# Half tiles of x2 instead of whole tiles between the counts of the dst tiles

## The chip, the cores and the metric

The kernel runs on one core of one Trainium2 chip. The time is the device time of one execution in microseconds (us), as the median of several runs; lower is better. A profile of one execution stands beside it.

## The reference, cut to what matters

A graph layer over N = 1250 nodes with D = 1024 features and E = 20000 edges, sorted by dst:

```
xn = layernorm(x)
x  = x + gnn(xn, W, a, src, dst) + mix(xn, ...)[0]
x  = x + ffn(layernorm(x), ...)[0]

gnn: h = xn @ W;  e = exp(-leaky_relu(al[src] + ar[dst]))
     h'[n] = sum over edges with src == n of e * h[dst], divided by the sum of e
mix: x2 = layernorm(xn, ln1_g, ln1_b)
     q, k, v = x2 @ wq, x2 @ wk, x2 @ wv; a linear attention on cos and sin features, then its own ffn
```

The change lies in the first stage. It does two things that have nothing to do with each other but share the engines. It counts, for each pair (dst, src), how many edges there are (the gnn sums are later made as dense products with these counts), and it makes x2, transposed and split in a high and a low part for the products with wv, wk and wq.

## The kernel before, in words

The stage is `count_and_second_norm`. Nodes are in NT = 10 tiles of T = 125. Each engine has its own instruction stream, written out by hand, and semaphores tie them.

Counting. Edges are in 160 chunks of 125. For dst tile t, only the chunks that may hold a dst of this tile are gone through, in a loop that takes HOT = 3 chunks a turn. For each chunk VectorE (DVE) writes a one-hot of the src (`hot_s`, L399, 125x1250) and a one-hot of the dst within the tile (`hot_d`, L401), in one of three slots, after waiting on `s_used` that the slot is free. TensorE (PE) waits on `s_hot` for the chunk and multiplies the two in three matmuls (L468) that add up in `p_cnt[t % 2]`, three PSUM banks; this frees the slot (`s_used`). Three matmuls with zero operands open the sums (L461) and three close them (L472, `s_tile`). ScalarE (ACT) then copies the counts out in three pieces (`keep_counts`, L300, `s_kept`), and SyncE stores them.

x2. ACT has normalised the rows into `xr` (L305, `s_z`). For node tile i, PE transposes eight 125x128 blocks (L451) into `p_t`, which has two PSUM banks: blocks 0 to 3 go to bank 0, blocks 4 to 7 to bank 1 (`s_t` after each bank). ACT applies gain and bias, four activations per bank (`affine`, L316), into `x2[i % 2]` (`s_x2` after each bank), and copies the whole tile rounded as the high part (L321, `s_hi`). DVE subtracts for the low part (`keep_lo`, L387, `s_lo`). PE may write a bank again when `affine` has read it:

```
if i:
    pe.wait_ge(s_x2, 2 * i - 1 + half)
```

and `affine(i)` waits for `keep_lo(i - 2)`, whose buffer it takes.

Order. A table says which node tiles are transposed after the count of dst tile t:

```
AFTER = {0: (), 1: (0,), 2: (1, 2), 3: (3, 4), 4: (5,), 5: (6,), 6: (7,), 7: (8,), 8: (9,), 9: ()}
```

PE does `count_tile(t)`, then the transposes of `AFTER[t]`. ACT does `keep_counts(t)`, then `affine` of each tile of `AFTER[t]`, then waits for the next count. DVE does the one-hots of tile t, then `keep_lo` of the tiles of `AFTER[t - 1]`, then the one-hots of t + 1. "Gap t" below is the time between the chunks of dst tile t and those of t + 1.

After tile 9, ACT and DVE finish the last x2 tile and a barrier ends the stage; the products with wv, wk and wq (L1468) follow.

Of the kernel before, what the change touches and what calls it, by code (L numbers as in the profile page):

```python
# [6 lines left out]
ACT = mybir.ActivationFunctionType  # L7
# [10 lines left out]
T = 125  # L18
NT = N // T
T16 = T // 16 * 16  # L20
MOVED = 32
K8 = D // 128
# [106 lines left out]
def count_and_second_norm(core):  # L129
# [3 lines left out]
    x2_hi, x2_lo = core.x2_hi, core.x2_lo  # L133
    with ExitStack() as ctx:  # L134
# [6 lines left out]
        xr = sb("x_rows", [T, NT, D])  # L141
# [65 lines left out]

        RSTD_STEPS = 26

        AFTER = {0: (), 1: (0,), 2: (1, 2), 3: (3, 4), 4: (5,), 5: (6,), 6: (7,), 7: (8,), 8: (9,), 9: ()}  # L210

        block = ctx.enter_context(nc.Block())

# [68 lines left out]
        @block.scalar  # L282
        def _(act):
            def first_stats(i):
                col = slice(i, i + 1)
                act.wait_ge(s_x[i], MOVED)
                act.wait_ge(s_stat, 3 * i)
                act.activation(junk[:], xr[:, i, :], ACT.Identity, accum_out=core.mean[:, col]).then_inc(s_stat, 1)
                act.wait_ge(s_stat, 3 * i + 1)
                act.mul(core.negmean[:, col], core.mean[:, col], -1.0 / D).then_inc(s_stat, 1)  # L290
                act.wait_ge(s_stat, 3 * i + 2)
                act.activation(junk[:], xr[:, i, :], ACT.Square, bias=core.negmean[:, col],
                               accum_out=core.var[:, col]).then_inc(s_stat, 1)

            def keep_counts(t):
                act.wait_ge(s_tile, t + 1)
                if t >= 2:
                    act.wait_ge(s_cst[t % 2], MOVED * (t // 2))
                for n, (a, w) in enumerate(THIRDS):
                    last = act.activation(kept(t)[:, a:a + w], p_cnt[0:T, t % 2, n, 0:w], ACT.Copy)  # L300
                last.then_inc(s_kept, 1)

            def normalise(i):
                col = slice(i, i + 1)
                act.activation(xr[:, i, :], xr[:, i, :], ACT.Identity, scale=core.ln_scale[:, col],  # L305
                               bias=core.ln_shift[:, col]).then_inc(s_z, 1)

            def affine(i):
                if i >= 2:
                    act.wait_ge(s_lo, i - 1)  # L310
                for k in range(K8):
                    if k % 4 == 0:
                        act.wait_ge(s_t, 2 * i + k // 4 + 1)
                    g = core.cols[:, COLUMN_AT["L0_mix_ln1_g"].start + k:COLUMN_AT["L0_mix_ln1_g"].start + k + 1]
                    b = core.cols[:, COLUMN_AT["L0_mix_ln1_b"].start + k:COLUMN_AT["L0_mix_ln1_b"].start + k + 1]
                    last = act.activation(x2[:, i % 2, k, :], p_t[:, k // 4, (k % 4) * T:(k % 4 + 1) * T], ACT.Identity,  # L316
                                          scale=g, bias=b)
                    if k % 4 == 3:
                        last.then_inc(s_x2, 1)
                act.wait_ge(s_x2, 2 * i + 2)  # L320
                act.activation(x2_hi[:, :, i * T:(i + 1) * T], x2[:, i % 2], ACT.Copy).then_inc(s_hi, 1)  # L321

            for i in range(NT):
                first_stats(i)
            keep_counts(0)
            act.wait_ge(s_rstd, RSTD_STEPS)
            for i in range(NT):
                normalise(i)
                if i == 3:
                    keep_counts(1)  # L330
            act.wait_ge(s_gb, 1)
            for t in range(2, NT):
                for i in AFTER[t - 1]:
                    affine(i)
                keep_counts(t)
                if t == NT - 2:
                    for which in range(3):
                        act.wait_ge(core.mix_loaded[which], 16)
                        act.activation(core.mix_hi[which][:], core.mix_in[which][:], ACT.Copy).then_inc(core.mix_hi_ready[which], 1)

        @block.vector
        def _(dve):
# [46 lines left out]
            with dve.register("chunks_done") as done, dve.register("first_chunk") as r0, dve.register("past_chunk") as r1:  # L389
                dve.reg_mov(done, 0)  # L390

                def tile_onehots(t):
                    first, past = groups_of(dve, t, (r0, r1))
                    with dve.Fori(first, past, HOT) as g:
                        before = dve.snap(done, min_val=0, max_val=NT * (CHUNKS + HOT))
                        for j in range(HOT):
                            dve.wait_ge(s_used, before + j + 1)
                            at = bass.ds(g + j, 1)
                            dve.tensor_scalar(hot_s[:, j, :], iota_h[:], ends[:, at, 0:1].rearrange("p a b -> p (a b)"), None,  # L399
                                              ALU.is_equal)  # L400
                            dve.tensor_scalar(hot_d[:, j, 0:T], iota_t[:, t, 0:T], ends[:, at, 1:2].rearrange("p a b -> p (a b)"),  # L401
                                              None, ALU.is_equal).then_inc(s_hot, 1)
                        dve.reg_add(done, done, HOT)

                tile_onehots(0)
                dve.wait_ge(s_vt, 1)
                dve.tensor_copy(core.cols[:], p_cols[:, 0:COLUMN_COUNT]).then_inc(s_gb, 1)
                tile_onehots(1)
                for t in range(2, NT):
                    for i in AFTER[t - 2]:  # L410
                        keep_lo(i)
                    tile_onehots(t)
                for i in AFTER[NT - 2]:
                    keep_lo(i)
                dve.wait_ge(core.mix_hi_ready[VALUE], 1)
                dve.tensor_tensor(core.mix_lo[VALUE][:], core.mix_in[VALUE][:], f32(core.mix_hi[VALUE][:]),
                                  ALU.subtract).then_inc(core.mix_lo_ready[VALUE], 1)

        @block.tensor
        def _(pe):  # L420
# [18 lines left out]
            pe.wait_ge(s_zero, 2)  # L439
            pe.wait_ge(s_span, 1)  # L440

            def transposes(i):
                pe.wait_ge(s_z, i + 1)
                if i == 0:
                    pe.wait_ge(s_gb, 1)
                for half in range(2):
                    if i:
                        pe.wait_ge(s_x2, 2 * i - 1 + half)
                    for n in range(4):
                        k = 4 * half + n  # L450
                        last = pe.transpose(p_t[:, half, n * T:(n + 1) * T], xr[:, i, k * 128:(k + 1) * 128], ident[0:T, 0:T])  # L451
                    last.then_inc(s_t, 1)

            with pe.register("chunks_done") as done, pe.register("first_chunk") as r0, pe.register("past_chunk") as r1:
                pe.reg_mov(done, 0)

                def count_tile(t):
                    if t >= 2:
                        pe.wait_ge(s_kept, t - 1)
                    for n, (a, w) in enumerate(THIRDS):  # L460
                        pe.matmul(p_cnt[0:T, t % 2, n, 0:w], zeros[:], zero_rows[:, 0:w], start=True, stop=False)  # L461
                    first, past = groups_of(pe, t, (r0, r1))
                    with pe.Fori(first, past, HOT):
                        before = pe.snap(done, min_val=0, max_val=NT * (CHUNKS + HOT))
                        for j in range(HOT):
                            pe.wait_ge(s_hot, before + j + 1)
                            for n, (a, w) in enumerate(THIRDS):
                                last = pe.matmul(p_cnt[0:T, t % 2, n, 0:w], hot_d[:, j, 0:T], hot_s[:, j, a:a + w], start=False, stop=False)  # L468
                            last.then_inc(s_used, 1)
                        pe.reg_add(done, done, HOT)  # L470
                    for n, (a, w) in enumerate(THIRDS):
                        last = pe.matmul(p_cnt[0:T, t % 2, n, 0:w], zeros[:], zero_rows[:, 0:w], start=False, stop=True)  # L472
                    last.then_inc(s_tile, 1)

                count_tile(0)
                pe.wait_ge(core.vectors_loaded, 16 * len(COLUMNS))
                pe.transpose(p_cols[:, 0:COLUMN_COUNT], core.vectors[:], ident[0:COLUMN_COUNT, 0:COLUMN_COUNT]).then_inc(s_vt, 1)
                for t in range(1, NT):
                    count_tile(t)
                    for i in AFTER.get(t, ()):  # L480
                        transposes(i)


def node_features(core):
# [2005 lines left out]
```

## Time and profile before

| | |
|---|---|
| time, median of 3 runs | 1284.93 us (1282.96 to 1285.98) |
| the profiled execution, its own time | 1283.55 us |
| its span in the profile | 1281.8 us |
| PE busy | 1196.6 us, 93% of the span |
| DVE busy | 756.2 us, 59% |
| ACT busy | 705.5 us, 55% |
| counting stage | up to about 156 us of the span |

The span starts with the first instruction of the profile. In timelines each row has its start, its duration, engine, line, and in brackets how long the engine had been idle and who ended that. PEld is the load of weights on TensorE, which overlaps its matmuls.

### The profile page before, as it was taken

How to read it: one execution, taken by the hardware profiler on the slowest of the kernel's cores; microseconds unless marked ns; L12 is line 12 of the kernel's file. 1: busy time of each engine (PE TensorE's matmuls, PEld its weight loads, DVE VectorE, ACT ScalarE, POOL GpSimd, SP SyncE). 2: the span in 40 equal slices, each digit the busy share in tenths (PEclk: the TensorE clock that was granted, in tenths of full speed). 3: DMA queues.
4: the chain of work that ended last, by engine and by line, in shares of the span. 5: the costliest groups of instructions: out<-in, count | busy, mean ns of one | idle time of the engine just before them, and what ended most of it. 6: DMA issues, size and time to landing. Idle time of an engine off the chain costs nothing. (4 is left out here: it accounts for less than half of the span.)

```text
span 1281.8 us, 19485 instructions
## 1 busy us (share of the span) xinstructions
PE 1196.6 (93%) x6857; PEld 1050.0 (82%) x6857; DVE 756.2 (59%) x1244; ACT 705.5 (55%) x1069; POOL 338.4 (26%) x296
## 2 busy tenths in 40 slices
PE   6989889999999999999559998899999998999997
PEld 4555689999999999999547876899988786887884
DVE  7988815656565666656543664777755122556646
ACT  8275628777777777777755432322245432355544
POOL 1500004242332324242111110266653332111100
PEclk9999999999999999999759999899998999999999
DMA  8001220022020202021145452522244332711103
GB/s 215 10 20 29 46 77 1 18 53 69 0 69 0 69 0 69 4 65 64 55 150 168 159 167 95 186 84 85 84 118 158 97 96 60 221 44 47 34 19 97
DMA packets 72194, 99.41 MB, mean 78 GB/s; under 512 B 27241, under 2 KB 52165, under 8 KB 71631
## 3 DMA queue, kind: packets, MB, share of 16 engines
q1 hardware_dynamic: 68684, 86.11, 23.1%
q0 software_dynamic: 3456, 12.58, 3.2%
q8 instruction: 34, 0.56, 0.2%
q14 instruction: 20, 0.16, 0.0%
HBM read 77.04 MB, written 21.63 MB: 77 GB/s over the span
## 5 line engine op out<-in xcount | busy, mean ns | idle before, releaser
L1146 POOL TENSOR_TENSOR cos_sin_lo<-cos_sin,cos_sin_hi 125x1024 fp32r<-125x1024 f32 (+1 forms) x40 | 95.4, 2384 | 248.6 <-ACT cos_sin_hi L1234 248.6
L468 PE MATMUL p_cnt<-hot_s,hot_d 125*125 125x418 bf16 x540 | 112.7, 359 | 1.8 <-DVE hot_d L401 1.8
L705 PE MATMUL p_h<-x 128*125 128x512 f32 x400 | 110.3, 403 | 0.0
L399 DVE TENSOR_SCALAR hot_s<-iota_h,ends 125x1250 bf16<-125x1250 f16 x180 | 97.6, 542 | 14.4 <-PE p_cnt L468 12.3
L1468 PE MATMUL p_w<-x,mix_hi_v 128*128 128x416 f32 (+1 forms) x384 | 105.2, 355 | 0.0
L468 PEld LDWEIGHTS p_cnt<-hot_s,hot_d 125*125 125x125 bf16 x540 | 62.4, 138 | 51.5 <-DVE hot_d L401 41.4
L1468 PE MATMUL p_w<-x,mix_hi_q 128*128 128x416 f32 (+1 forms) x384 | 104.2, 352 | 0.0
L1468 PE MATMUL p_w<-x,mix_hi_k 128*128 128x416 f32 (+1 forms) x384 | 104.1, 352 | 0.0
L966 PE MATMUL rows_in_psum<-h_hi,a_lo 125*125 125x342 f32 x300 | 96.7, 322 | 2.7 <-DVE a_lo L910 2.7
L966 PE MATMUL rows_in_psum<-h_lo,a_hi 125*125 125x342 f32 x300 | 96.7, 322 | 0.0
L966 PE MATMUL rows_in_psum<-h_hi,a_hi 125*125 125x342 f32 x300 | 96.7, 322 | 0.0
L705 PEld LDWEIGHTS p_h<-x 128*125 128x125 f32 x400 | 75.4, 190 | 18.3
L1234 ACT ACTIVATE cos_sin_hi<-cos_sin 125x1024 fp32r<-125x1024 f32 (+1 forms) x80 | 83.6, 1045 | 7.0 <-PE p_kv_at L1549 4.8
L1376 DVE TENSOR_SCALAR whole_turns<-p_p 125x512 f32<-125x512 f32 (+1 forms) x80 | 54.6, 682 | 40.2 <-PE p_p L1519 35.3
L1800 PE MATMUL rows_in_psum<-wo_rest,at_hi 128*125 128x512 f32 x280 | 76.8, 396 | 0.0
L1219 ACT ACTIVATE cos_sin<-part_turn 125x512 f32<-125x512 f32 (+1 forms) x80 | 49.9, 623 | 48.8 <-DVE part_turn L1378 47.9
L1468 PEld LDWEIGHTS p_w<-x,mix_hi_v 128*128 128x128 f32 x384 | 73.1, 191 | 0.8
L1468 PEld LDWEIGHTS p_w<-x,mix_hi_q 128*128 128x128 f32 x384 | 72.1, 188 | 0.9
L1468 PEld LDWEIGHTS p_w<-x,mix_hi_k 128*128 128x128 f32 x384 | 72.2, 188 | 0.6
L1468 PE MATMUL p_w<-x,mix_lo_v 128*128 128x416 f32 (+1 forms) x192 | 69.0, 359 | 3.5 <-PEq L134 3.5
L1468 PE MATMUL p_w<-x,mix_lo_q 128*128 128x416 f32 (+1 forms) x192 | 67.6, 352 | 0.0
L1468 PE MATMUL p_w<-x,mix_lo_k 128*128 128x416 f32 (+1 forms) x192 | 67.6, 352 | 0.0
(297 smaller groups left out, 3055.6 us busy)
## 6 DMA issues: line engine op xcount, KB each, us to landing
x_in<-in_x_dram SPq DMA_DIRECT2D x30, 448.0 KB
attn_dram<-attn_t SPq DMA_DIRECT2D x8, 625.0 KB, 3.9
at_in<-attn_dram SPq DMA_DIRECT2D x10, 500.0 KB, 4.6
x_rows<-in_x_dram SPq DMA_DIRECT2D x10, 448.0 KB
x_in<-gnn_dram SPq DMA_DIRECT2D x10, 448.0 KB
out_dram<-rows SPq DMA_DIRECT2D x10, 448.0 KB
mix_in_v<-in_L_mix_wv_dram SPq DMA_DIRECT2D x8, 512.0 KB, 6.0
mix_in_k<-in_L_mix_wk_dram SPq DMA_DIRECT2D x8, 512.0 KB, 4.7
```

The lines of the kernel that those rows point to most:

```text
L399: dve.tensor_scalar(hot_s[:, j, :], iota_h[:], ends[:, at, 0:1].rearrange("p a b -> p (a b)"), None, ALU.is_equal)
L468: last = pe.matmul(p_cnt[0:T, t % 2, n, 0:w], hot_d[:, j, 0:T], hot_s[:, j, a:a + w], start=False, stop=False)
L705: last = pe.matmul(p_h[0:T, i % 2, n, :], left[i % 2][:, k, :], right[:, k, cols], start=(k == 0 and m == 0), stop=(k == K8 - 1 and m == 2))
L966: last = pe.matmul(p_o[0:T, i % 2, n, 0:H_COLS], left[:, i % 2, d, :], right[:, d, cols], start=(d == 0 and m == 0), stop=(d == NT - 1 and ...
L1146: pool.tensor_tensor(full(cs_lo, k), full(cs, k), f32(full(cs_hi, k)), ALU.subtract).then_inc(s_cslo[0], 1)
L1219: act.activation(step_view(cs, k, 1), rows(part, k), ACT.Sin, scale=TWO_PI)
L1234: act.activation(full(cs_hi, k), full(cs, k), ACT.Copy).then_inc(s_cshi, 1)
L1376: dve.tensor_scalar(flat(whole, k), flat(p_p, k), MAGIC, -MAGIC, ALU.add, ALU.add).then_inc(s_whole, 1)
L1468: last = pe.matmul(p_w[:, n, 0:w], left[which][:, k, :], right[:, k, a:a + w], start=(k == 0 and m == 0), stop=(k == K8 - 1 and m == 2))
L1800: last = pe.matmul(p_o[i % 2][0:T, n, :], left[i % 2][:, k, :], right[:, n * 512:(n + 1) * 512], start=(k == 0 and m == 0), stop=(k == K8 ...
```

## The change

The unit of the table becomes half a tile, u = 2 * i + half, that is one PSUM bank of four blocks. 20 units go into the gaps as 2, 3, 3, 3, 3, 2, 2, 2. Before, in the same units, it was 2, 4, 4, 2, 2, 2, 2, 2. The high and the low part stay whole tiles and go with the second half.

```diff
-        AFTER = {0: (), 1: (0,), 2: (1, 2), 3: (3, 4), 4: (5,), 5: (6,), 6: (7,), 7: (8,), 8: (9,), 9: ()}
+        AFTER = {0: (), 1: (0, 1), 2: (2, 3, 4), 3: (5, 6, 7), 4: (8, 9, 10), 5: (11, 12, 13), 6: (14, 15), 7: (16, 17), 8: (18, 19), 9: ()}
...
-            def affine(i):
-                if i >= 2:
+            def affine(u):
+                i, half = divmod(u, 2)
+                if i >= 2 and half == 0:
                     act.wait_ge(s_lo, i - 1)
-                for k in range(K8):
-                    if k % 4 == 0:
-                        act.wait_ge(s_t, 2 * i + k // 4 + 1)
+                act.wait_ge(s_t, u + 1)
+                for k in range(4 * half, 4 * half + 4):
...
-                    if k % 4 == 3:
-                        last.then_inc(s_x2, 1)
-                act.wait_ge(s_x2, 2 * i + 2)
-                act.activation(x2_hi[:, :, i * T:(i + 1) * T], x2[:, i % 2], ACT.Copy).then_inc(s_hi, 1)
+                last.then_inc(s_x2, 1)
+                if half:
+                    act.wait_ge(s_x2, u + 1)
+                    act.activation(x2_hi[:, :, i * T:(i + 1) * T], x2[:, i % 2], ACT.Copy).then_inc(s_hi, 1)
...
-                    for i in AFTER[t - 2]:
-                        keep_lo(i)
+                    for u in AFTER[t - 2]:
+                        if u % 2:
+                            keep_lo(u // 2)
                     tile_onehots(t)
...
-            def transposes(i):
+            def transposes(u):
+                i, half = divmod(u, 2)
                 pe.wait_ge(s_z, i + 1)
                 if i == 0:
                     pe.wait_ge(s_gb, 1)
-                for half in range(2):
-                    if i:
-                        pe.wait_ge(s_x2, 2 * i - 1 + half)
+                else:
+                    pe.wait_ge(s_x2, u - 1)
+                for n in range(4):
```

## Rows read from the trace of the kernel before

**Rows 1.** The page: the head, and the costliest line of DVE in the stage

```profile
span 1281.8 us, 19485 instructions
...
L399 DVE TENSOR_SCALAR hot_s<-iota_h,ends 125x1250 bf16<-125x1250 f16 x180 | 97.6, 542 | 14.4 <-PE p_cnt L468 12.3
```

**Rows 2.** Waits, 62 to 172 us: engine, line, for whom, total us, times, longest

```profile
PEld p_cnt L468 <- DVE hot_d L401: 21.6, 86, 0.6
DVE hot_s L399 <- PE p_cnt L468: 11.7, 8, 4.8
PE p_t L451 <- ACT x_rows L316: 5.4, 4, 2.0
```

**Rows 3.** Timeline of DVE around gaps 2, 3, 4, 5 and 6

```profile
77.40 0.25 DVE L401 TENSOR_SCALAR hot_d<-iota_t,ends 125x125 bf16<-125x125 f16 x1
...
85.04 0.55 DVE L399 TENSOR_SCALAR hot_s<-iota_h,ends 125x1250 bf16<-125x1250 f16 x1 [3.76 <-PE p_cnt L468]
...
92.47 2.30 DVE L387 TENSOR_TENSOR x<-x_rows,x 128x1000 fp32r<-128x1000 f32 x2
...
101.42 0.55 DVE L399 TENSOR_SCALAR hot_s<-iota_h,ends 125x1250 bf16<-125x1250 f16 x1 [4.78 <-PE p_cnt L468]
...
108.85 2.29 DVE L387 TENSOR_TENSOR x<-x_rows,x 128x1000 fp32r<-128x1000 f32 x2
...
112.93 0.53 DVE L399 TENSOR_SCALAR hot_s<-iota_h,ends 125x1250 bf16<-125x1250 f16 x1
...
118.50 1.18 DVE L387 TENSOR_TENSOR x<-x_rows,x 128x1000 fp32r<-128x1000 f32 x1
...
121.97 0.55 DVE L399 TENSOR_SCALAR hot_s<-iota_h,ends 125x1250 bf16<-125x1250 f16 x1 [0.43 <-PE p_cnt L468]
...
127.54 1.20 DVE L387 TENSOR_TENSOR x<-x_rows,x 128x1000 fp32r<-128x1000 f32 x1
```

**Rows 4.** Timeline of PE: gap 2, the transposes of gap 5, the stage's end

```profile
78.82 1.02 PE L451 MATMUL p_t<-ident,x_rows 125*128 125x125 f32 x8
81.88 0.62 PE L451 MATMUL p_t<-ident,x_rows 125*128 125x125 f32 x4 [2.04 <-ACT x_rows L316]
83.17 0.65 PE L451 MATMUL p_t<-ident,x_rows 125*128 125x125 f32 x4 [0.68 <-ACT x_rows L316]
...
119.74 1.02 PE L451 MATMUL p_t<-ident,x_rows 125*128 125x125 f32 x8
...
156.00 0.69 PE L1468 MATMUL p_w<-x,mix_lo_v 128*128 128x418 f32 x1 [3.53 <-PEq L134]
```

**Rows 5.** Timeline of PE's weight loads, gaps 2 and 3

```profile
81.85 0.41 PEld L451 LDWEIGHTS p_t<-ident,x_rows 125*128 125x128 f32 x4 [2.25 <-issue]
83.17 0.41 PEld L451 LDWEIGHTS p_t<-ident,x_rows 125*128 125x128 f32 x4 [0.91 <-ACT x_rows L316]
83.55 0.42 PEld L461 LDWEIGHTS p_cnt<-zero_rows,zeros 125*125 125x125 bf16 x3
84.01 1.56 PEld L468 LDWEIGHTS p_cnt<-hot_s,hot_d 125*125 125x125 bf16 x9
...
98.08 0.71 PEld L451 LDWEIGHTS p_t<-ident,x_rows 125*128 125x128 f32 x4 [0.91 <-ACT x_rows L316]
...
99.67 2.36 PEld L468 LDWEIGHTS p_cnt<-hot_s,hot_d 125*125 125x125 bf16 x9
```

**Rows 6.** Timeline of ACT in gap 2

```profile
79.02 1.34 ACT L300 ACTIVATE x_in<-p_cnt 125x418 uint16<-125x418 f32 x3 [0.83 <-PE p_cnt L472]
80.23 2.89 ACT L316 ACTIVATE x_rows<-p_t,columns 128x125 f32<-128x125 f32 x8
83.15 1.04 ACT L321 ACTIVATE x<-x_rows 128x1000 fp32r<-128x1000 f32 x1
```

**Rows 7.** Busy us (x) by engine in three stretches; then clock, DMA share, GB/s

```profile
83.00:86.00 3.00, 2.83 (x17) 2.19 (x18) 0.96 (x3) 2.97 (x8) 0.00 (x0) 1.00 0.05 9
98.00:101.00 3.00, 2.92 (x10) 2.27 (x11) 0.00 (x0) 2.97 (x8) 0.00 (x0) 0.50 0.01 2
...
180.00:200.00 20.00, 15.69 (x96) 14.71 (x95) 8.20 (x12) 11.48 (x18) 2.42 (x1) 1.00 0.00 1
```

**Rows 8.** Timeline of PE in the next stage, two pauses

```profile
187.03 0.56 PE L1493 MATMUL p_tr<-ident,v_t 128*125 128x128 f32 x3 [1.70 <-DVE v_both L1349]
188.85 0.67 PE L1493 MATMUL p_tr<-ident,v_t 128*125 128x128 f32 x4 [1.26 <-DVE v_both L1349]
```

More of the change, by code:

```diff
@@ L332, in _ @@
             for t in range(2, NT):
-                for i in AFTER[t - 1]:
-                    affine(i)
+                for u in AFTER[t - 1]:
+                    affine(u)
                 keep_counts(t)
@@ L409, in _ @@
                 for t in range(2, NT):
-                    for i in AFTER[t - 2]:
-                        keep_lo(i)
+                    for u in AFTER[t - 2]:
+                        if u % 2:
+                            keep_lo(u // 2)
                     tile_onehots(t)
-                for i in AFTER[NT - 2]:
-                    keep_lo(i)
+                for u in AFTER[NT - 2]:
+                    if u % 2:
+                        keep_lo(u // 2)
                 dve.wait_ge(core.mix_hi_ready[VALUE], 1)
@@ L445, in transposes @@
                     pe.wait_ge(s_gb, 1)
-                for half in range(2):
-                    if i:
-                        pe.wait_ge(s_x2, 2 * i - 1 + half)
[L449 to L452, printed above, removed]
+                else:
+                    pe.wait_ge(s_x2, u - 1)
+                for n in range(4):
+                    k = 4 * half + n
+                    last = pe.transpose(p_t[:, half, n * T:(n + 1) * T], xr[:, i, k * 128:(k + 1) * 128], ident[0:T, 0:T])
+                last.then_inc(s_t, 1)
             with pe.register("chunks_done") as done, pe.register("first_chunk") as r0, pe.register("past_chunk") as r1:
@@ L479, in _ @@
                     count_tile(t)
-                    for i in AFTER.get(t, ()):
-                        transposes(i)
+                    for u in AFTER.get(t, ()):
+                        transposes(u)
 def node_features(core):
```

## The prediction

> **What bounds the stage now.** I read the page first, then the waits of the stage, then the timelines of DVE, PE, the weight loads and ACT around each gap between two dst tiles, and last the granted clock. The span is 1281.8 us [rows 1]; the profiled execution took 1283.55 us by its own time, 1.75 us more, and the median of the three runs is 1284.93 us, 1.38 us above that execution.
>
> Inside a dst tile DVE sets the pace. TensorE's weight loads for the counts waited 86 times for DVE's one-hots, 21.6 us together, never over 0.6 us [rows 2]. DVE writes the pair of one-hots of a chunk every 0.62 us. So the tiles themselves cost the same before and after, and only the gaps count. In them it is DVE that waits for PE: 11.7 us in 8 waits, the longest 4.8 us [rows 2]. The reader should see where that comes from. DVE may write three chunks ahead, then needs a slot back, and PE gives the first one back only when it is through its transposes, the three opening matmuls and the first chunk.
>
> I therefore measure a gap on DVE, from the end of the issue of the last one-hot of tile t (which is where `keep_lo` starts when its input is there) to the start of the fourth chunk of tile t + 1. In gap 2 the last `hot_d` starts at 77.40 and takes 0.16 us of DVE's issue, so 77.56; the fourth chunk starts at 85.04: 7.48 us. Gap 3: 92.47 to 101.42, 8.95 us. Gap 4: 108.85 to 112.93, 4.08 us. Gap 5: 118.50 to 121.97, 3.47 us [rows 3]. Gaps 6, 7 and 8 repeat gap 5 (one node tile each), and gap 1 is not touched.
>
> Gaps 2 and 3 are long because they hold two node tiles. The first eight transposes run at once; the next four write a bank that `affine` has still to read, and PE idles 2.04 us; the last four idle another 0.68 us [rows 4]. Both waits are for ACT, which begins with `keep_counts` (79.02 to 80.23) and only then does eight activations in 2.89 us [rows 6]. Gap 4 has one node tile on PE but two `keep_lo` on DVE, and there DVE alone is the length: 2.22 us for the two, then three chunks. Gap 5 has one of each, and PE is the length by a little.
>
> **The change, part by part.** The instructions are the same in number and shape: 80 transposes, 80 activations, 10 high parts, 10 low parts. Nothing is saved; what moves is the number of units in a gap.
>
> A gap of three units. Units one and two find their banks free, since `affine` of the gap before is over. Unit three takes the bank of unit one, so it waits for `keep_counts`, then the four activations of unit one: exactly the first wait of a gap of four. The same row prices it: its weights load at 81.85, 4.29 us after 77.56 [rows 5]. Behind it no second wait stands. The opening matmuls follow the last four transposes by 83.55 - 83.17 = 0.38 us, the first chunk by another 84.01 - 83.55 = 0.46 us, and DVE's fourth chunk comes 85.04 - 84.01 = 1.03 us later [rows 3, 5]. Sum: 4.29 + 0.38 + 0.46 + 1.03 = 6.16 us. On DVE such a gap holds one or two `keep_lo` and three chunks, at most 4.08 us as gap 4 shows, so they are covered and PE is the length.
>
> What queues behind that wait: on PE, in order, the rest of the transposes, the opening matmuls and every chunk of the next tile; DVE waits for those after three chunks, and nobody makes this up, because the tile behind it runs at DVE's pace.
>
> Gap by gap, against the profiled execution:
> Gap 2, from four units to three: 7.48 to 6.16, -1.32 us.
> Gap 3, from four to three: 8.95 to 6.16, -2.79 us. Of this 1.32 us is again the fourth unit. The other 1.47 us is the clock: the granted clock was 0.50 from 98 to 101 us, the 1.2 GHz level, against 1.00, the 2.4 GHz level, in the same place of gap 2 [rows 7]. From the last load of transposes to the first chunk it took 1.59 us in place of 0.84, and from there to DVE's fourth chunk 1.75 in place of 1.03 [rows 3, 5].
> Gap 4, from two to three: 4.08 to 6.16, +2.08 us.
> Gap 5, from two to three: 3.47 to 6.16, +2.69 us.
> Gap 6 keeps two units but gets two `keep_lo`, since the second halves of tiles 5 and 6 (units 11 and 13) both fell in gap 5: 3.47 to 4.08, +0.61 us.
> Gaps 1, 7, 8: 0.
> Sum: -1.32 - 2.79 + 2.08 + 2.69 + 0.61 = +1.27 us with the clock at full speed in all four gaps of three.
>
> Costed at nothing. ACT's own load: after a gap of three it has 1.21 of `keep_counts`, 3 x 1.45 of `affine` and up to two high parts of 0.95, 7.5 us, begun about 1.5 us into the gap; the shortest distance to the next gap is that of gap 5 to 6, 127.54 - 118.50 = 9.04 us [rows 3] plus the added 2.69, so it is over before. If it were not, `keep_counts` would come late by the difference. The waits on `s_lo`: `affine` of unit 8 needs the low part of tile 2, which DVE now makes at the start of the same gap, done 1.1 us in, while ACT is still in `keep_counts`. The stores of the counts have a whole tile's time. The end of the stage after tile 9 is the same chain; the next stage begins behind the barrier, at 156.00 [rows 4], and shifts as a whole. I see nothing in it that runs by its own clock and would absorb the shift.
>
> **Where the Trainium skill speaks against the change.** The trace shows PE's clock fall once, after pauses of 2.04 and 0.68 us with only four transposes between, and not fall after the same pair in gap 2, nor after pauses of 1.70 and 1.26 us in the next stage, where the clock stays at 1.00 from 180 to 200 us [rows 4, 7, 8]. So one 2.04 us pause, as in the new gaps, is milder than three cases of which one fell. The Trainium skill, page "TensorE: Matmul & The Clock Gate", section "A second HAM failure mode: psum-queue depth-cycling", says that small pauses of PE between groups of matmuls, when buffers in PSUM are cycled, can make the clock swing between its levels again and again. By that rule four gaps with a pause would be worse than two; by the rows they are not clearly so.
>
> **The rivals.**
> B. The clock falls in one of the four gaps. It is as in gap 3 before: +1.47 us, in all +2.74 us against the profiled execution, 1287.7 us on the median.
> C. The clock falls in two to four of them, the swinging clock. +4.2 to +7.2 us, 1289.1 to 1292.1 us. For it: four pauses of 2.04 us instead of two. Against it: the second pause, 0.68 us, is gone from each.
> D. The other side: the third unit doesn't wait, because the pause in gap 2 is owed to something else than the bank (a late start of ACT, say). Then a gap of three is 3.47 plus 0.46 us of transposes, 3.93 us, or 4.08 where DVE has two low parts. The gaps change by -3.55, -5.02, 0, +0.46 and +0.61, that is -7.5 us, 1277.4 us. It decides where the wait shrinks: at 2.04 - 1.27 / 4 = 1.72 us there is no change, and below about 1.08 us the kernel is faster by over 0.2%. Against it: the wait ends with `affine`, and ACT goes from 80.23 straight on [rows 6].
> E. The change is not seen: other work takes the slack, or runs differ by more. 1284.9 us. The three runs before lie 3 us apart, about two clock falls; if the median run had a second fall in gap 2, then the same sum from it is near zero.
>
> **How the numbers follow.** The likeliest is the sum with no fall, +1.27 us on the median: 1286.2 us. Chances: this 0.50, B 0.22, C 0.12, D 0.05, E 0.11. A measurement of this kernel can tell about 0.2%, 2.6 us, from no change. B lies just at this bound and is halved between same and slower. Slower: 0.11 of B, 0.12 of C and 0.03 of the first make 0.26. Faster: D, 0.05, and 0.01 for a before with two falls and an after with none. Same: 0.68. The range goes down to 1283.8, which is the sum on the profiled execution, 1284.82, less 1 us for the spread of the runs, and up to 1289.6, which is two falls (+4.2 us on the median, 1289.1) and a little. Beyond it lie D and most of C's upper part.
>
> **What would show it.** In the profile after: PE's four transposes of unit three preceded by a pause of about 2.0 us for ACT in gaps 2, 3, 4 and 5, and no pause of 0.68 us; DVE waiting for a slot 2.4 us in gap 2 (in place of 3.76), 3.1 us in gaps 3 and 5 (in place of 4.78 and 0.43) and 2.0 us in gap 4 (none before); two `keep_lo` in a row before tiles 5 and 7; the first matmul of the next stage at 157.3 us in place of 156.00, or 1.5 us later for each stretch of 0.50 clock. The prediction is wrong if the pauses are shorter than 1.7 us, if a pause of 2 us pulls the clock down each time, or if the later stages don't shift along.

## The result, and the profile after

| | before | changed |
|---|---|---|
| median | 1285.71 us (7 runs, 1282.96 to 1289.98) | 1293.31 us (7 runs, 1288.41 to 1295.95) |
| ratio to before | | 1.0052, 95% interval 1.003 to 1.0075 |
| the profiled execution, its own time | 1283.55 us | 1288.41 us |
| its span | 1281.8 us | 1286.6 us |
| first matmul of the next stage | 156.00 us | 160.78 us |

The change makes the kernel about 0.5% slower, by 3.9 to 9.6 us going by the interval. In a later series, with more runs, the same kernel stood at 1.004 (1.0023 to 1.0057), 5 us (experiment e1). The forecast was 1286.2 us, with 1289.6 us as the upper end, and slower by over 0.2% had only 0.26. The direction of its sum, +1.27 us, was right and the size was not. The two profiled executions differ by 4.8 us of span, and all of it arises before 160.78 us; behind that point both kernels take the same time. The profiled execution of the changed kernel is the fastest of its seven, so the profile shows less than the median lost.

The DVE timeline of the changed kernel, at the same places as [rows 3]:

```profile
84.93 0.55 DVE L399 TENSOR_SCALAR hot_s<-iota_h,ends 125x1250 bf16<-125x1250 f16 x1 [2.83 <-PE p_cnt L470]
...
92.36 1.19 DVE L387 TENSOR_TENSOR x<-x_rows,x 128x1000 fp32r<-128x1000 f32 x1
...
98.94 0.55 DVE L399 TENSOR_SCALAR hot_s<-iota_h,ends 125x1250 bf16<-125x1250 f16 x1 [3.53 <-PE p_cnt L470]
...
106.36 2.31 DVE L387 TENSOR_TENSOR x<-x_rows,x 128x1000 fp32r<-128x1000 f32 x2
...
112.92 0.55 DVE L399 TENSOR_SCALAR hot_s<-iota_h,ends 125x1250 bf16<-125x1250 f16 x1 [2.39 <-PE p_cnt L470]
...
118.49 1.19 DVE L387 TENSOR_TENSOR x<-x_rows,x 128x1000 fp32r<-128x1000 f32 x1
...
125.61 0.55 DVE L399 TENSOR_SCALAR hot_s<-iota_h,ends 125x1250 bf16<-125x1250 f16 x1 [4.06 <-PE p_cnt L470]
126.08 0.25 DVE L401 TENSOR_SCALAR hot_d<-iota_t,ends 125x125 bf16<-125x125 f16 x1
126.67 0.55 DVE L399 TENSOR_SCALAR hot_s<-iota_h,ends 125x1250 bf16<-125x1250 f16 x1 [0.34 <-PE p_cnt L470]
...
131.77 2.30 DVE L387 TENSOR_TENSOR x<-x_rows,x 128x1000 fp32r<-128x1000 f32 x2
...
135.85 0.54 DVE L399 TENSOR_SCALAR hot_s<-iota_h,ends 125x1250 bf16<-125x1250 f16 x1
```

The reader should see the forecast's pattern with its numbers a little off. DVE now waits for a slot after every gap of three: 2.83, 3.53, 2.39 and 4.06 us, where 2.4, 3.1, 2.0 and 3.1 were forecast. Two `keep_lo` in a row stand at 106.36 and 131.77, as forecast. Gap 6 takes 135.85 - 131.77 = 4.08 us, as forecast. Gaps 3 and 4 take 6.58 and 6.56 us, and gap 2 takes 6.56 too, counted as in the prediction, where 6.16 was forecast.

The PE timeline of the changed kernel, gaps 2, 3 and 5, against [rows 4]:

```profile
79.63 1.02 PE L453 MATMUL p_t<-ident,x_rows 125*128 125x125 f32 x8
82.70 0.62 PE L453 MATMUL p_t<-ident,x_rows 125*128 125x125 f32 x4 [2.05 <-ACT x_rows L316]
83.15 0.69 PE L463 MATMUL p_cnt<-zero_rows,zeros 125*125 125x418 bf16 x3
84.03 9.21 PE L470 MATMUL p_cnt<-hot_s,hot_d 125*125 125x418 bf16 x45 [0.19 <-issue]
...
96.68 0.62 PE L453 MATMUL p_t<-ident,x_rows 125*128 125x125 f32 x4 [2.05 <-ACT x_rows L316]
...
122.82 0.62 PE L453 MATMUL p_t<-ident,x_rows 125*128 125x125 f32 x4 [2.05 <-ACT x_rows L316]
```

The pause is 2.05 us in each gap of three and the 0.68 us pause is gone. New is the 0.19 us of "issue" ahead of the first chunk. The weight loads of the same kernel show it better, against [rows 5]:

```profile
82.67 0.41 PEld L453 LDWEIGHTS p_t<-ident,x_rows 125*128 125x128 f32 x4 [2.25 <-issue]
83.05 0.42 PEld L463 LDWEIGHTS p_cnt<-zero_rows,zeros 125*125 125x125 bf16 x3
84.03 1.44 PEld L470 LDWEIGHTS p_cnt<-hot_s,hot_d 125*125 125x125 bf16 x9 [0.56 <-issue]
```

From the opening matmuls to the first chunk it is 84.03 - 83.05 = 0.98 us; the forecast took 0.46 us from before. The clock in gaps 2, 3, 4 and 5 of the changed kernel (busy by engine, then granted clock, DMA share, GB/s), against [rows 7]:

```profile
82.00:86.00 4.00, 3.11 (x18) 2.17 (x19) 1.17 (x4) 3.97 (x11) 0.00 (x0) 1.00 0.40 82
97.00:101.00 4.00, 3.78 (x22) 2.27 (x20) 2.06 (x7) 3.97 (x10) 0.00 (x0) 1.00 0.18 36
111.00:115.00 4.00, 3.81 (x22) 2.30 (x21) 2.08 (x7) 3.35 (x8) 0.00 (x0) 1.00 0.18 36
123.00:127.00 4.00, 4.00 (x16) 2.62 (x15) 1.05 (x3) 3.97 (x10) 0.00 (x0) 0.57 0.21 42
```

One fall, in gap 5. It makes the gap 125.61 - 118.49 = 7.12 us and keeps PE behind DVE in tile 6 for another 0.6 us (125.61 to 131.77 is 6.16 us; 121.97 to 127.54 in [rows 3] is 5.57).

So the 4.8 us between the two executions are: +0.8 us before gap 2 (tile 1 began at 50.45 us instead of 49.62; in the twelve kernels below it began anywhere from 49.5 to 51.1, and the change has no part in it), gap 2 -0.92, gap 3 -2.37, gap 4 +2.48, gap 5 +3.64 and +0.6 behind it, gap 6 +0.58. Sum +4.8.

### The profile page after: what moved, and what is told of

Its sections match the earlier page's. It is cut to its first block and busy times, and to the rows that moved or that the text cites. A ratio compares the mean times of both kernels' runs of the same rounds, so it can differ in the third digit from the quotient of the medians.

```text
span 1286.6 us, 19495 instructions
## 1 busy us (share of the span) xinstructions
PE 1197.0 (93%) x6857; PEld 1049.1 (82%) x6857; DVE 756.8 (59%) x1244; ACT 705.6 (55%) x1069; POOL 337.1 (26%) x296
```

## The experiments

Two things were open: the 0.4 us more in each gap of three, and why the median lost more than the profile shows. A "fall" is a stretch in which the granted clock is 0.50. Theory F: the clock falls more often in the changed kernel, and not in the same gaps from run to run. Theories S and R: the load of PE's registers, which stands behind the long wait, comes late, by S because PE has two waits there and by R because of its own length. The code lines shown as removed are those of the changed kernel. "Gap" is measured on DVE as in the prediction.

**e1, the changed kernel again.** No edit.

> The changed kernel once more, for the distribution of its times and a second profile. Theory F (clock falls): its profile showed one stretch at 0.50 clock in the counting stage, in gap 5, and that run was the fastest of seven (1288.4 us against a median of 1293.3); a slower run should show two or more such stretches after gaps of three units, each worth about 1.2 to 1.5 us in the distance between the first matmuls of tile 2 and the first matmul of the next stage (92.5 us in the first profile). Rival G: the stage is as long as in the first profile, 160.8 us to its end, and the time is lost elsewhere.

Measured: 1289.47 us (10 runs), ratio 1.004 (1.0023 to 1.0057). Its profiled execution took 1290.13 us and the next stage began at 162.41 us. The clock of the same kernel in gap 2's place, gap 3's, 4's and 5's:

```profile
82.00:86.00 4.00, 3.80 (x23) 2.30 (x20) 2.06 (x7) 3.37 (x8) 0.00 (x0) 1.00 0.20 41
97.00:101.00 4.00, 3.95 (x13) 2.69 (x14) 2.15 (x6) 3.43 (x8) 0.00 (x0) 0.57 0.00 1
111.00:115.00 4.00, 3.90 (x14) 2.95 (x15) 0.63 (x2) 3.77 (x9) 0.00 (x0) 0.57 0.28 55
123.00:127.00 4.00, 2.58 (x10) 1.88 (x11) 0.16 (x1) 3.97 (x11) 0.00 (x0) 0.73 0.39 78
```

Three falls, in gaps 3, 4 and 5, against one in the first profile. Each costs in the gap or in the tile behind it: 1.4, 1.2 and 1.2 us over a gap of 6.56 us and a tile at DVE's pace. From the first chunk of tile 1 (on DVE) to the first matmul of the next stage it is 112.95 us, against 110.33 in the first profile. Theory F holds as far as two profiles go: the clock of the same kernel falls once or three times.

**e2, PE waits for the rows once.**

```diff
-                pe.wait_ge(s_z, i + 1)
-                if i == 0:
+                if u == 0:
+                    pe.wait_ge(s_z, 1)
                     pe.wait_ge(s_gb, 1)
-                else:
+                elif u == 2:
+                    pe.wait_ge(s_z, NT)
+                if u:
                     pe.wait_ge(s_x2, u - 1)
```

> PE waits for the normalised rows once instead of before every half tile. Theory S (a second wait on the same matmul blocks PE's instruction stream, so that the register load and the loop's head behind the four transposes are no longer run ahead, seen as 0.56 us of issue between the opening matmuls and the first chunk): the gaps of three shrink from 6.56 to about 6.16 us, 1.6 us in all, and the 0.56 us of issue is gone. Rival: the 0.56 us is the register load's own length after any wait and stays; no change against the changed kernel.

Measured: gaps of three 6.55, 6.58, 6.61 us (and 7.24 with a fall), 0.61 to 0.67 us of issue ahead of the first chunk where there is no fall. Median 1292.5 us (6 runs), ratio 1.0057 (1.0035 to 1.0079). Theory S fell: the second wait has no part in it.

**e3, the new code with the old table.**

```diff
-        AFTER = {0: (), 1: (0, 1), 2: (2, 3, 4), 3: (5, 6, 7), 4: (8, 9, 10), 5: (11, 12, 13), 6: (14, 15), 7: (16, 17), 8: (18, 19), 9: ()}
+        AFTER = {0: (), 1: (0, 1), 2: (2, 3, 4, 5), 3: (6, 7, 8, 9), 4: (10, 11), 5: (12, 13), 6: (14, 15), 7: (16, 17), 8: (18, 19), 9: ()}
```

> The changed code (half tiles as units, a wait for the rows before each) with the table of before, in units 2, 4, 4, 2, 2, 2, 2, 2. If only the distribution over the gaps matters: the time of before, gaps 2 and 3 at 7.5 us (9.0 with a fall of the clock). If the second wait per half tile costs by itself: gaps 2 and 3 at 7.9 us, in all +0.8 us against before. If the restructured code costs elsewhere: more than that.

Measured: 1286.02 us (12 runs), ratio 1.0012 (0.9995 to 1.0029), not told from before. Gap 2 is 7.55 us, gap 3 9.03 us with a fall, as in the first profile of before, and the weight loads have no idle time of 0.56 us there. So the table makes the loss; rewriting the code in half tiles costs at most 0.1 us a gap.

**e4, the pause filled.**

```diff
-                    for u in AFTER.get(t, ()):
+                    for n, u in enumerate(AFTER.get(t, ())):
+                        if n == 2:
+                            pe.wait_ge(s_kept, t)
+                            for _ in range(4):
+                                for m, (c, w) in enumerate(THIRDS):
+                                    pe.matmul(p_cnt[0:T, (t + 1) % 2, m, 0:w], zeros[:], zero_rows[:, 0:w], start=True, stop=True)
                         transposes(u)
```

> The changed kernel with TensorE kept busy in the pause of each gap of three: twelve matmuls with zero operands into the counts' free banks, about 2.1 us, before the third unit (they add nothing to the counts, which are opened anew afterwards). They lie in a pause of 2.05 us, so they cost at most 0.3 us a gap. Theory F: no stretch of 0.50 clock in the counting stage after them, and a median lower than the changed kernel's by the falls it has, 1.5 us each, up to 5 us. Rival G (the time is lost elsewhere, or falls are not owed to the pauses): same or slower than the changed kernel by up to 1.2 us.

Measured: 1285.99 us (12 runs), ratio 1.0012 (0.9998 to 1.0027). PE timeline of gap 3 of this kernel, and below it the clock from gap 2 to gap 5:

```profile
93.50 1.02 PE L453 MATMUL p_t<-ident,x_rows 125*128 125x125 f32 x8
94.35 2.28 PE L487 MATMUL p_cnt<-zero_rows,zeros 125*125 125x418 bf16 x12
96.56 0.62 PE L453 MATMUL p_t<-ident,x_rows 125*128 125x125 f32 x4
97.02 0.69 PE L463 MATMUL p_cnt<-zero_rows,zeros 125*125 125x418 bf16 x3
...
```

```profile
84.00:88.00 4.00, 4.00 (x21) 2.37 (x21) 3.20 (x11) 2.26 (x5) 0.00 (x0) 1.00 0.02 4
98.00:102.00 4.00, 4.00 (x21) 2.40 (x21) 3.17 (x11) 3.30 (x8) 0.00 (x0) 1.00 0.00 0
111.00:115.00 4.00, 3.81 (x21) 2.29 (x20) 2.17 (x7) 3.26 (x8) 0.00 (x0) 1.00 0.17 33
122.00:126.00 4.00, 3.81 (x23) 2.48 (x22) 1.03 (x3) 3.97 (x11) 0.00 (x0) 1.00 0.41 82
```

The twelve matmuls fill the pause and delay nothing: the gaps are 6.58, 6.61, 6.58 and 6.57 us, as they were without a fall. No fall is left in them. From the first chunk of tile 1 to the next stage it is 109.25 us, against 110.33 with one fall and 112.95 with three (e1). The median is 3.5 us under e1 on the same chip. Work was added and the kernel became faster; what it took away from this stage is the falls. That is theory F. If the whole difference of the medians is owed to them, the falls of the changed kernel are worth about 3.5 us in the median run.

**e5, the register load ahead of the transposes.** Each count begins with a load of the tile's first and last chunk into PE's registers.

```diff
-                def count_tile(t):
+                def count_tile(t, ahead=None):
...
-                    first, past = groups_of(pe, t, (r0, r1))
+                    first, past = ahead or groups_of(pe, t, (r0, r1))
...
+                ahead = None
                 for t in range(1, NT):
-                    count_tile(t)
+                    count_tile(t, ahead)
+                    if t + 1 < NT:
+                        ahead = groups_of(pe, t + 1, (r0, r1))
```

> The changed kernel with PE's register load of the next tile's first and last chunk moved ahead of the transposes. The gaps of three measured 6.56 us where 6.16 was forecast; PE idled 0.56 us (its weight loads) between the opening matmuls and the first chunk. Theory R (after a wait that stops PE's instruction stream, the register load's own time lies bare): the 0.56 us shrinks and the gaps are 6.16 to 6.3 us. Rival: it is the fetch of the instructions behind the wait, or the loop's head; the gaps stay at 6.56 us.

Measured in one run: gaps 3 and 4 at 6.16 and 6.17 us. Gaps 2 and 5 had falls, which cost 1.6 and 1.5 us with the tile behind them. The two without a fall are the forecast's 6.16. Theory R holds: the missing 0.4 us a gap is the register load, which lies bare behind the pause. The run took 1286.37 us; one time says nothing of the median.

**e6, ACT turns the first unit before it keeps the counts.**

```diff
+        EARLY = {3: 1}
...
-                for u in AFTER[t - 1]:
+                for u in AFTER[t - 1][EARLY.get(len(AFTER[t - 1]), 0) if t > 2 else 0:]:
+                    affine(u)
+                for u in AFTER[t][:EARLY.get(len(AFTER[t]), 0)]:
                     affine(u)
                 keep_counts(t)
```

> The changed kernel, but in the gaps of three ACT does affine of the first unit before it keeps the counts. The wait of the third unit then ends after the first unit's transposes and its four activations: 0.8 us earlier, pause about 1.25 us in place of 2.05. Stall theory: gaps of three 5.75 us, 3.2 us less in the four, and fewer falls of the clock, so 3.2 to 6 us under the changed kernel, about level with before. Rival: the counts, kept later, delay the opening matmuls or the low parts, and the gaps stay over 6.3 us.

Measured: gaps of three 5.36, 5.37, 5.41 and 5.37 us, 1.2 us less and not 0.8, and no fall in them. Median 1284.99 us (10 runs), ratio 0.9995 (0.9978 to 1.0013), level with before as forecast. PE's timeline shows the pause, and its weight loads that nothing is bare behind it now:

```profile
95.38 0.62 PE L457 MATMUL p_t<-ident,x_rows 125*128 125x125 f32 x4 [1.25 <-ACT x_rows L318]
```

```profile
95.35 0.41 PEld L457 LDWEIGHTS p_t<-ident,x_rows 125*128 125x128 f32 x4 [1.45 <-issue]
95.73 0.42 PEld L467 LDWEIGHTS p_cnt<-zero_rows,zeros 125*125 125x125 bf16 x3
96.22 1.53 PEld L474 LDWEIGHTS p_cnt<-hot_s,hot_d 125*125 125x125 bf16 x9
```

So the wait is the cause of the gap's length: it ends 0.8 us sooner and the gap is 0.8 us shorter, plus the 0.4 us of the register load, which is covered again. Why the load is bare behind a pause of 2.05 us and not behind one of 1.25 us, these runs don't tell.

**e7, the same with the old table** (e3 with `EARLY = {4: 2}` and the loop of e6).

> The table of before in half tiles, with ACT doing affine of the first two units of a gap of four before it keeps the counts. By the stalls: gaps 2 and 3 at 6.8 us in place of 7.5, pauses of 1.25 and 0.7 us; 1.4 us under before, and another 1 to 1.5 us where before has a fall of the clock. Rival: no difference from the kernel before beyond 1 us.

Measured: 1282.97 us (10 runs), ratio 0.9965 (0.9948 to 0.9982). Gap 2 was 6.75 us, as forecast. Gap 3 had a fall and took 7.40 us, although its pauses were only 1.31 and 0.77 us. By the ratio the kernel is 4.5 us under before, where 2.4 to 2.9 were forecast; the surplus isn't explained.

**e8, the old table with the pause filled** (e3 with the filling of e4).

> The table of before in half tiles, with twelve zero matmuls in the first pause of gaps 2 and 3. If before's median holds falls of the clock too: no stretch of 0.50 in the counting stage, gaps 2 and 3 both at about 7.5 us, and a median 1 to 2 us under before. If before has a fall only in a minority of its runs: same within 0.7 us.

Measured: 1283.66 us (10 runs), ratio 0.9981 (0.9969 to 0.9992). Gaps 2 and 3 are 7.56 and 7.54 us, without a fall. From the first chunk of tile 1 to the next stage it is 105.02 us, against 106.38 in the profile of before, which has one fall. By the ratio the filling gains 2.4 us, by the medians on this chip 2.8. So the typical run of before has falls as well, one or two if the whole gain is owed to them.

**e9, the changed kernel with e4 and e5 together.**

> The changed kernel with the register load moved ahead of the transposes and the pause of each gap of three filled by zero matmuls: the forecast's sum of +2.74 us against a before without falls of the clock, with its two missing terms taken out. Stall theory: four gaps at 6.16 us, no 0.50 clock in the counting stage, and 2.5 to 2.7 us above the old table with the same filling (the run beside it), about level with the kernel before, whose runs have falls. Rival: some cost of the change is still not named; over 4 us above the old table with filling.

Measured: 1284.66 us (12 runs), ratio 1.0 (0.9986 to 1.0014). The gaps are 6.16, 6.16, 6.16 and 6.17 us, then 4.07, and no fall in any. Weight loads of gap 3:

```profile
93.11 2.00 PEld L490 LDWEIGHTS p_cnt<-zero_rows,zeros 125*125 125x125 bf16 x12
95.40 0.41 PEld L453 LDWEIGHTS p_t<-ident,x_rows 125*128 125x128 f32 x4 [0.28 <-issue]
95.78 0.42 PEld L463 LDWEIGHTS p_cnt<-zero_rows,zeros 125*125 125x125 bf16 x3
96.23 1.56 PEld L470 LDWEIGHTS p_cnt<-hot_s,hot_d 125*125 125x125 bf16 x9
```

0.38 us from the third unit to the opening matmuls and 0.45 us from these to the first chunk: the forecast's terms.

**e10, the kernel of e8 beside it.**

> The table of before in half tiles with its first pauses filled, once more beside the run above on the same chip. It should again be 2 to 3 us under the kernel before, which would be the worth of the falls of the clock in that kernel's own runs. Rival: the first result was chance; same as before within 1 us.

Measured: 1282.96 us (12 runs), ratio 0.9989 (0.9973 to 1.0005), 1.7 us under e9; the gaps of the two profiles differ by 39.24 - 36.69 = 2.55 us in sum, forecast 2.5 to 2.7. Against before its gain is 1.4 us by the ratio and 2.7 by the medians, and its interval includes 1: by itself it is not told from no gain. With e8, the falls of the kernel before are worth 1.4 to 2.8 us, no closer.

**e11, the new table with all three cures** (e5, e6, and six zero matmuls in the pause).

> The changed table with all three cures: affine of the first unit before the counts are kept, the register load ahead, six zero matmuls in what is left of the pause. Gaps of three at 4.95 to 5.05 us. By the sum of gaps 34.4 us against 36.4 for before without falls and 37.9 to 39 with them: 2 us under before and another 2 to 3 for the falls, so 0.3 to 0.4% faster. Rival: DVE or ACT becomes the bound and the gaps stay over 5.3 us.

Measured: 1283.56 us (12 runs), ratio 0.9983 (0.9967 to 0.9998), a gain of 0.17% where 0.3 to 0.4% was forecast. The gaps stay at 5.37, 5.37, 5.45 and 5.38 us, a miss of 0.4 us each: e6 had already covered the register load, and it can't be taken out twice.

**e12, the old table with all three.**

> The table of before with the same three cures (two units before the counts are kept). Gaps 2 and 3 at 6.75 us: the register load is not bare there, since the short second pause ends on the last unit. Sum of gaps 35.1 us: 1.3 us under before without falls, and 2 to 3 for the falls, 0.25 to 0.35% faster, within 1 us of the run above. Rival: level with e8 (the filling alone).

Measured: 1280.41 us (11 runs), ratio 0.9956 (0.9943 to 0.9969), the fastest of all kernels here, 5.7 us or 0.44% under before by the ratio, where 0.25 to 0.35% was forecast. Gaps 2 and 3 are 6.77 and 6.81 us, both at full clock; the third line is a stretch of the next stage:

```profile
80.00:84.00 4.00, 3.04 (x20) 2.17 (x19) 1.22 (x4) 3.97 (x10) 0.00 (x0) 1.00 0.00 0
94.00:98.00 4.00, 2.98 (x20) 2.11 (x19) 1.84 (x6) 3.97 (x11) 0.00 (x0) 1.00 0.00 0
186.00:194.00 8.00, 6.55 (x28) 6.27 (x29) 4.73 (x8) 5.12 (x7) 0.00 (x0) 0.57 0.01 2
```

It is 3.1 us under e11, where within 1 us was forecast and the gaps of the two profiles differ by 36.15 - 35.21 = 0.94 us. The spans of the two profiles are the same, 1280.6 us. So the other 2.2 us are not in the gaps, and they aren't explained.

What was won in the counting stage was in part lost in the next. Between the first matmul of that stage and the first one that makes `p_kv_at` from `kv_both`, the instructions are the same in all kernels. Before, they start at 156.00 [rows 4] and 228.74 us, 72.7 us apart:

```profile
228.74 0.28 PE L1549 MATMUL p_kv_at<-cos_sin_lo,kv_both 128*128 128x250 f32 x1
```

In e12 they are 75.3 us apart:

```profile
153.08 0.69 PE L1482 MATMUL p_w<-x,mix_lo_v 128*128 128x418 f32 x1 [3.54 <-PEq L134]
...
228.35 0.28 PE L1563 MATMUL p_kv_at<-cos_sin_lo,kv_both 128*128 128x250 f32 x1
```

Of the 2.9 us that e12 is ahead at 153.08 us, 0.4 us are left at 228.35. The distance is 72.7 to 72.9 us in the profiles of before, changed and e1 to e6, 73.9 and 74.1 in e7 and e10, and 74.9 to 75.4 in e8, e9, e11 and e12. From 180 to 200 us the granted clock is 1.00 in the first eight and 0.83 in the last six.

The table gives the sum of gaps 1 to 8 beside the median. Sums from one profile each; a fall's part in the tile behind a gap is not in them.

| kernel | falls in the gaps | sum of gaps, us | ratio to before |
|---|---|---|---|
| before | 1 | 37.98 | 1 |
| changed | 1 | 41.36 | 1.0052 |
| changed, e1 | 3 | 42.73 | 1.004 |
| e4, changed, filled | 0 | 40.90 | 1.0012 |
| e9, changed, filled, register load ahead | 0 | 39.24 | 1.0 |
| e8, old table, filled | 0 | 36.65 | 0.9981 |
| e6, changed, ACT first | 0 | 36.04 | 0.9995 |
| e12, old table, all three | 0 | 35.21 | 0.9956 |

## Why the prediction was wrong

**The pause of the third unit** was forecast at about 2.0 us and is 2.05 us in all four gaps. The chain behind the prediction's 6.16 us is right term by term, as e9 shows, and e6 shows that the wait makes the gap: shorten it and the gap shrinks by as much. Rival D is out.

**Gaps 4, 5 and 6** took from the shift what was forecast, but for the terms below: two gaps paid for a third unit, one for a second `keep_lo` (4.08 us, as forecast).

**First failed step: "the first chunk by another 84.01 - 83.55 = 0.46 us".** It was taken from a gap of four, where a short second pause follows the long one. In a gap of three it is 0.98 us in the weight loads, which lengthens the gap by 0.40 us, four times, 1.6 us in all. What lies bare is PE's register load ahead of the count's loop: moved ahead of the transposes (e5) it takes the gap to 6.16 us. The forecast had no term for the register load: in the row that it took its 0.46 us from, the load was covered.

**Second failed step: "one 2.04 us pause, as in the new gaps, is milder than three cases of which one fell", and the 0.50 given to no fall.** The first profile has one fall, e1 three of four possible, e2 one and e5 two. Filling the pauses lowers the changed kernel's median by 3.5 us; at 1.1 to 1.6 us a fall that is two or three falls in its median run, an estimate. The sample of before was one execution, and the clock falls in the same place in some runs and not in others. The prediction gave little weight to what the Trainium skill says ("TensorE: Matmul & The Clock Gate", section "A second HAM failure mode: psum-queue depth-cycling"): small pauses between groups of matmuls can make the clock swing. The traces agree, with one to three falls in four gaps. Rival C, the swinging clock, stood at 1289.1 to 1292.1 us with a chance of 0.12. With the 1.6 us of the register load it would be 1290.7 to 1293.7 us, which holds the median 1293.31 us but only 5 of the 17 runs of the changed kernel, and not the median of e1, 1289.47 us.

**A term that the baseline hid.** The sum counted -1.47 us for a fall that the profiled execution of before had in gap 3, and set no fall against it after. But that fall was no exception. By medians and ratios, before has falls worth 1.4 to 2.8 us and the changed kernel 3.5 us. Without falls on either side the table costs 40.90 - 36.65 = 4.25 us in the gaps: the forecast's 2.74 and the 1.6 of the register load make 4.34. With 0.7 to 2.1 us more for falls it is 5.0 to 6.4 us, and the two ratios say 5.1 and 6.7. The profiles say the same of the stage alone: from the first chunk of tile 1 to the next stage it is 106.38 us before, with one fall, and 110.33 and 112.95 us in the changed kernel with one and with three, 3.9 and 6.6 us more.

**Rival E** had a true part: runs of either kernel lie 7 us apart, and part of this is the falls. Why a run has more or fewer of them is not settled. Two other parts are seen in the profiles. The first 73 to 75 us of the next stage take up to 2.7 us more in e7 to e12, where the clock falls there too; whether an earlier start of that stage or something else brings this on was not tested. And the work from the first matmul with `kv_both` to the end, 1053.0 us before and in the changed kernel, took 1049.7 to 1053.3 us in the fourteen profiles, with no order by kernel that was found. So the lengths of gaps are shown to a few hundredths, while what a fall is worth in the median of a kernel is argued from medians that hold these parts too.

## What to carry to other kernels

A buffer that must be read back before it can be written again costs its wait each time it comes round in one gap. Spreading the work evenly multiplied the long first wait instead of the short one that follows it: the third unit of a gap costs 6.56 - 3.47 = 3.1 us (2.7 without the register load), the fourth only 7.48 - 6.56 = 0.9 us more; put the units where the long wait is already paid, and shorten that wait by the order on the engine that reads the buffer.

Look past the stage that was changed before a gain in it is booked: here up to 2.7 us of it went again in the next 75 us.

When a sum is made against one profiled execution, take out of both sides what that execution met by chance (a fall of the clock), and price it as a chance for each place that can have it. A cost found in one neighbourhood (0.46 us behind a short pause) needs a look at what the neighbourhood was covering.

## What the runs showed of the hardware

TensorE's clock went to the 1.2 GHz level (0.50) in or after pauses of about 2 us (1.95 to 2.05) that stood alone between busy stretches in 7 of 16 gaps: one of four in the first profile of the changed kernel and in e2, two in e5, three in e1. After a lone pause of 1.25 to 1.31 us it fell in none of four (e6), but it fell once after pauses of 1.31 and 0.77 us (e7, gap 3). Twelve matmuls with zero operands in the long pause (2.28 us) kept it at 1.00 in all twelve gaps of the profiles that had them (e4, e8, e9, e10), at no cost in the gap's length (6.58 us against 6.56).

A fall cost 1.1 to 1.6 us although it lasted through a stretch in which DVE sets the pace. At the lower level PE falls behind DVE: nine weight loads, three chunks, took 2.36 us after the fall in gap 3 and 1.56 us in gap 2 [rows 5], that is 0.79 us a chunk at the 1.2 GHz level and 0.52 at 2.4 GHz, where DVE writes one every 0.62 us.

PE's load of two register values before a loop cost 0.4 us after a wait of 2.05 us, with the pause empty or filled by matmuls (6.56 and 6.58 us), and nothing that shows after a wait of 1.25 us or when it stood ahead of the wait.
